# Second attention layer: the value matmuls of a group in one burst of eight key tiles, and a ring of twelve probability buffers

## The reference, cut to what matters

```
scores = einsum('bhqd,bhkd->bhqk', q, k)
R = E[clip(pos_k - pos_q, -127, 127) + 127]
scores = scores + einsum('bhqd,kqd->bhqk', q, R)
attn = softmax(scores, axis=-1)
out = einsum('bhqk,bhkd->bhqd', attn, v)
```

## Time and profile before

| | |
|---|---|
| median of 3 runs | 1829.59 us (1827.02 to 1834.72) |
| profiled execution, its time | 1839.94 us |
| its span | 1838.2 us |
| PE busy | 1478.4 us (80%) |
| DVE / ACT / POOL busy | 1027.7 / 859.8 / 697.0 us |
| L1001 (exponentials), 512 | 285.5 us busy, from 1110.6 us to 1744.9 us |
| L845 (values), 4096 records | 170.3 us busy |
| L858 (fold), 8 records of one group at 1378.91 us | 1.08 us |
| granted clock, 1480 to 1613 us | 1.00 |
| granted clock, 1613 to 1620 us | 0.52 |

### The profile page before, as it was taken

One profiled execution on the slowest core, in us unless ns is written; L12 is line 12 of the kernel. 1 busy time (PEld: TensorE's weight loads), 2 busy tenths in 40 slices (PEclk: granted clock), 3 DMA queues, 4 the chain that ended last, 5 costly groups with the idle time before them and its releaser, 6 DMA issues. The chain is left out here.

```text
span 1838.2 us, 42125 instructions
## 1 busy us (share of the span) xinstructions
PE 1478.4 (80%) x15527; PEld 978.1 (53%) x15527; DVE 1027.7 (56%) x2775; ACT 859.8 (47%) x1544; POOL 697.0 (38%) x1372
## 2 busy tenths in 40 slices
PE   3799999968999995327994269999997699999935
PEld 2476666655666674315763145555555355555524
DVE  5656555484655655570231765666665566666553
ACT  2355455544554552000221146677764377767622
POOL 1266556524665661015355023333332234333300
PEclk9999999989999998558997567999997589999968
DMA  4000000000000000521343016676660367766400
GB/s 124 1 1 2 3 1 2 2 1 1 1 2 2 2 1 1 170 102 65 65 94 64 5 56 195 189 205 197 201 190 16 107 196 208 210 195 193 140 1 23
DMA packets 104953, 148.74 MB, mean 81 GB/s; under 512 B 13750, under 2 KB 61238, under 8 KB 104758
## 3 DMA queue, kind: packets, MB, share of 16 engines
q1 hardware_dynamic: 97974, 141.22, 26.0%
q0 software_dynamic: 6784, 4.87, 2.0%
HBM read 68.49 MB, written 77.21 MB: 79 GB/s over the span
## 5 line engine op out<-in xcount | busy, mean ns | idle before, releaser
L658 DVE CUSTOM_DVE_ANT_0 t_Z<-t_psS,a0b_L 128x1024 f32<-128x1024 f32 x256 | 311.1, 1220 | 185.4 <-issue 182.7
L716 ACT ACTIVATE t_Pt<-t_psT 128x512 f32<-128x512 f32 x512 | 278.6, 595 | 252.9 <-PE t_psT L614 252.9
L1001 ACT ACTIVATE t_Pt<-t_psT 128x512 f32<-128x512 f32 x512 | 285.5, 595 | 146.4 <-PE t_psT L819 86.9
L904 DVE TENSOR_REDUCE t_mm<-t_psS 128x1 f32<-128x640 f32 (+1 forms) x256 | 219.6, 858 | 221.6 <-DMA t_A<-relative_rows 160.2
L614 PE MATMUL t_psT<-idf,t_Z 128*128 128x128 f32 x2048 | 285.1, 283 | 8.3 <-POOL t_Z L681 4.7
L681 POOL TENSOR_SCALAR t_Z<-t_Z,t_m 128x1024 f32<-128x1024 f32 x256 | 287.3, 1122 | 0.0
L614 PEld LDWEIGHTS t_psT<-idf,t_Z 128*128 128x128 f32 x2048 | 225.9, 144 | 59.5 <-issue 32.1
L805 PE MATMUL t_psS<-a1b_KT,a1b_QT 72*128 72x384 bf16 (+3 forms) x864 | 224.5, 313 | 10.7 <-DVE t_mm L905 10.4
L991 ACT ACTIVATE t_rows<-t_psT 128x512 f32<-128x512 f32 x256 | 153.2, 599 | 49.4 <-PE t_psT L797 43.1
L845 PE MATMUL t_psO<-t_Pt,t_Vh 128*32 128x128 f32 x4096 | 170.3, 286 | 6.6 <-DVE t_Os L928 6.6
L588 PE MATMUL t_psO<-t_Pt,t_Vh 128*32 128x128 f32 x4096 | 164.6, 280 | 0.3 <-ACT t_Pt L716 0.3
(11 more groups left out here) (260 smaller groups left out, 1817.5 us busy)
## 6 DMA issues: line engine op xcount, KB each, us to landing
relative_rows<-t_rows SPq DMA_DIRECT2D x256, 256.0 KB, 3.0
t_A<-relative_rows SPq DMA_DIRECT2D x192, 192.0 KB, 3.4
t_A<-relative_rows SPq DMA_DIRECT2D x64, 128.0 KB, 2.8
x_B<-in_b SPq DMA_DIRECT2D x1, 4096.0 KB, 18.7
x_A<-in_a SPq DMA_DIRECT2D x1, 4096.0 KB, 27.0
a1b_QT<-t_mr SPq DMA_DIRECT2D x192, 1.0 KB
expert_rows<-zp SPq DMA_DIRECT2D x1, 2740.0 KB, 13.1
x_xe<-expert_rows SPq DMA_DIRECT2D x8, 342.5 KB, 3.0
```

Source lines behind the costliest of these rows:

```text
L658: nc.vector.tensor_tensor_reduce(out=Z[:, j, :], in0=psS[:, j % 2, :], in1=L[:, qt, :], scale=1.0, scalar=3e38, op0=ALU.add, op1=ALU.min, ...
L716: nc.scalar.activation(Pt[:, qt % 2, j, half * (N // 2):(half + 1) * (N // 2)], psT[:, half, :], ACT.Exp).then_inc(s_exp, 1)
L904: v.reduce_max(mm[:, u % AR, 1:2], psS[:, u % 2, width:N], AX)
L1001: nc.scalar.activation(Pt[:, q % PR, :], psT[:, unit_item(G, i) % RR, :], ACT.Exp).then_inc(s_exp, 1)
```

## The change

The ring `Pt` grows from six to twelve buffers. `values` of a group no longer follow in pairs behind every second unit: all eight come behind u1 and r0 of the next group. What is multiplied, and its order, stays as it was.

```diff
-    ZR, AR, PR, RR = 3, 8, 6, 3
+    ZR, AR, PR, RR = 3, 8, 12, 3
...
                             if i == 1 and G >= 1:
-                                values(G - 1, 6)
-                                values(G - 1, 7)
-                            if i > 1 and G >= 0:
-                                values(G, i - 3)
-                                values(G, i - 2)
+                                for n in range(QT_N):
+                                    values(G - 1, n)
...
-                values(GROUPS - 1, 6)
-                values(GROUPS - 1, 7)
+                for n in range(QT_N):
+                    values(GROUPS - 1, n)
```

## The result

The changed kernel takes 1859.85 us (median of five runs), the kernel before 1829.59 (median of five). The forecast was 11 us faster, 1818 us, and 1859.85 us lies above its range of 1797 to 1843 us. The execution that was profiled is the quickest of the five, 1835.32 us.

What follows compares the result with a forecast made beforehand. SP's loop (7.98 to 8.70 us a group) was taken to bound the kernel over a floor of 8.20 us. Groups of 8.50 for 8.68 us over some 62 groups save 11 us: 1829.59 to 1818 us, 8 in 10 between 1797 and 1843.

Steps and rivals of the forecast that it cites:

- What bounds the kernel: PE's list (7.92 us a group) and SP's loop (8.0 to 8.7 us) run nearly level, the second being slower.
- PE's own work: One burst of 64 records for four of 16 saves 0.66 us a group if PE alone set the pace.
- the full gain: Rival: PE's saving of 0.66 us a group comes through in full, 41 us, to 1789 us; chance 0.10.
- The three buffers: Between PE and ACT: ACT runs out of work during the burst, so a group's floor is 8.20 us, 0.28 us higher.
- falls into that slack in part: In every fourth group, which folds, PE's extra 1.0 us was to fall partly into the slack.
- The wait for `Os`: PE's wait for DVE's copy before the values of every fourth group goes, worth 0.17 to 0.28 us a group.
- the second rival: SP's loop sets the time as before, the `Os` wait being the same late `A`: 1825 to 1834 us; chance 0.30.
- The maxima: PE's wait for them at r2 can grow: only some 0.2 us left for a late `A`, now 0.4 us.
- The sum: SP's loop sets the group over a floor of 8.20 us: 8.50 us for 8.68, 11 us less over 62 groups.
- The slower rival: ACT starves behind the burst and r2 waits for the maxima: +0.36 us a group, +22 us, 1852 us; chance 0.20.
- The sign that the prediction named: The prediction would be wrong if the clock fell to 1.2 GHz more often than once in each batch.

Runs made afterwards that it cites:

- e5: The kernel before, with the three DMAs of the maxima issued by GpSimd and not by SP: 0.9931 of the kernel before, 1821.29 us.
- e10: The kernel before, with `A` fetched from an always-ready input, not the stored rows (relative term's values left out): 0.9728 of the kernel before, 1794.45 us.
- e4: The changed kernel with the whole burst one step later, behind u3 and r1, and `copy_out` one tile later: 1.0021 of the kernel before, 1849.26 us.
- e12: The kernel before, with the maxima's DMAs on GpSimd and the copy of `psO` to `Os` on ACT: 0.9929 of the kernel before, 1829.60 us.
- e1_again: The changed kernel, unaltered, measured again on another chip: 1.0087 of the kernel before, 1861.79 us; its profiled execution took 1859.95 us.
- e2: The kernel before with only the ring of twelve buffers, values still in pairs: 0.9987 of the kernel before, 1840.81 us.
- e11: The changed kernel, with `A` fetched from an always-ready input, not the stored rows (relative term's values left out): 0.9827 of the kernel before, 1812.27 us.
- e6: The changed kernel, with the three DMAs of the maxima issued by GpSimd and not by SP: 0.9964 of the kernel before, 1828.37 us.
- e8: The changed kernel with the burst behind r1 of the next group and the maxima's DMAs on GpSimd: 0.9965 of the kernel before, 1828.70 us.
- e13: The changed kernel with the burst behind r1 and `A` from an always-ready input (relative term's values left out): 0.9717 of the kernel before, 1785.91 us.
- e14: The changed kernel with values in two bursts of four key tiles and `A` from an always-ready input: 0.9789 of the kernel before, 1797.26 us.
- e9: The changed kernel with r1 of every group computed three times and r3 twice: 1.0115 of the kernel before, 1863.12 us.

## Why the prediction was wrong

**What bounds the kernel.** Both numbers were read rightly, PE's list at 7.92 us and SP's loop at 7.98 to 8.70 us; that the slower sets the group was not. In the trace of the kernel before, 19 of the 56 groups between the first and the last three of both batches are at PE's own floor (7.92 us inside, 7.61 at an edge, 9.08 with a fold), and the others lie above it by 42 us in all. Giving SP's loop slack saved 13 us (`e5`), removing nearly all late tiles 49 us (`e10`), and lowering the floor under late tiles nothing (`e4`).

**PE's own work.** Right: records of 64, 1.96 us, one exit of 0.20 us, 39.4 us less busy time on L845. The rule of the Trainium skill (TensorEngine Tiling (Array Packing), section Key Properties), by which six of eight drains go, agrees with the 0.20 us behind the burst; the full gain that it would give by itself did not come, since PE got no buffer to spend it in.

**The three buffers.** Right to 0.02 us at every step from the burst to the next, in an inner group. This part gave +0.28 us a group, by 62 groups 17 us, and the measured loss is 16 us with late tiles and 18 us nearly without. That agreement is luck. Only half of the groups are inner ones without a fold; the floor of an edge group rises by 0.17 us, and that of one with a fold falls by 0.22 us, as "falls into that slack in part" had it. The average rise is 0.12 us, or 7 us in all. The rest of the loss is time above the floor, for which the working had no term.

**The wait for `Os`.** It went, as said; sized at 0.17 to 0.28 us a group, no gain was measured (`e12`). That they were late tiles seen at another place is what the second rival had said, and this fits it.

**The maxima.** Over both batches PE's wait for them stayed, 44.9 us before and 45.0 us in `e1_again`; the growth in the window of 200 us was chance.

**The sum: the step that failed.** "The group is set by SP's loop, between 7.98 and 8.70 us, over a floor of 8.20 us" takes the larger of two paces. What the runs show in its place is a floor with late tiles on top. The 0.12 us of floor came through (7 us), although it lay under SP's loop, and the time above the floors didn't shrink but grew (39 to 50 us, `e2` to `e1_again`; 7 to 14 us, `e10` to `e11`). The gain of 0.18 us a group that the sum expected had no source: the higher floor wasn't hidden under SP's loop, and the wait for `Os` was worth nothing that could be measured. The median landing gave 8.70 us, which happened to be the average group of 8.68; that agreement was no evidence for a bound, since a floor with waits on top gives the same number. Why the time above the floor grows with the burst is argued, not shown: in `e1_again`'s timeline neither PE nor ACT has slack to take a late tile up within three buffers.

**The slower rival**, at 0.20 and +22 us, had the right side. Its price, near the 16 to 18 us by ratio, is partly luck: it is made of +0.28 us for the floor (0.12 on average), +0.30 us for the maxima (no growth) and -0.22 us for `Os` (nothing measured). Its first half, ACT starving behind the burst, is what the runs show. Its second, r2 waiting for the maxima, isn't needed: the loss is as large in `e11`, where that wait is no longer than in `e10` (12.6 us for 13.7 over both batches).

**The sign that the prediction named.** The clock did fall more often than once a batch, as "what would make the prediction wrong" had it: the granted clock over 1480 to 1740 us is 0.94 in `e1_again` and 0.99 in the kernel before. It was a weak sign, since the kernel before itself is at 0.96 over 1120 to 1380 us. `e11` has a loss of the same size at the clock of `e10`, so the loss doesn't need the clock. Whether it adds a few us where tiles are late, in bursts of 3.51 us like the one shown, stays open: no run changed the clock and nothing else.

**What stays open.** Why the time above the floor grows with the burst, and why `e6` lost less to it than `e1_again`, if it did. Why the late burst, with a floor 0.35 us lower, gains nothing (`e4`, `e8`, `e13`): against `e2`, `e4` saves 20 us of floors and has 74 us above them for 39. What a lower floor saved was lost above it, so the plain sum of floor and late tiles holds for the kernel before and the changed one, and not for every floor.

## What to carry to other kernels

When two engines pass work through few buffers, a saving on the first reaches the end only if the second still has something to work off: work out the group step by step from the start of the longest uninterrupted piece, and put such a piece ahead of the cheapest producers, not of the dearest. Work it out for each kind of group, and not only for the common one: 0.28 us was 0.12 on average. When a stage has both a floor and late inputs, don't take the larger pace; look how many groups already sit at the floor, and test with the inputs made always ready, before and after the edit. And what moves little but is cheap to try (three small DMAs off the busiest queue) beat the whole restructuring here, 0.7% faster against 1% slower.

## What the runs showed of the hardware

- A row of 64 value records is followed by an idle load engine for 0.20 us at the full clock, like one of 16 and those of 32 in `e14`.
- Issuing the three 1 KB transfers of the maxima holds SP's queue for 1.82 us, more than a fifth of a group; moved to GpSimd, which has time, it was worth 13 us.
- With extra matmuls in PE's pauses (`e9`) the granted clock rose from 0.94 to 0.98 in the second batch, stayed at 0.94 in the first, and the program took the same time (1.0115 for 1.0087). A granted clock by itself didn't tell what the time would be.
